# The first expert stage and the linear attention run as one stage, in slots of two tiles

## The chip, the cores and the metric

The kernel runs on one core of a Trainium2 chip. A core has TensorE for matrix products (PE in the profile, PEld for its weight loads), VectorE (DVE), ScalarE (ACT), GpSimd (POOL) and SyncE (SP), which here issues the transfers. Each engine works through its own instructions in order, and they meet through semaphores. The metric is the device time of one execution in microseconds; lower is better. Three runs of the kernel before gave 2261.31, 2261.96 and 2263.22 us, a median of 2261.96 us.

## The reference, cut to what matters

Four layers follow each other on x of 4 batches x 1024 tokens x 128 features. The change concerns the second and third step, of layers 0 and 1:

```
# experts of layer 0: E = 20, K = 2, H = 32
h = gelu(xf @ wg1 + bg1);  logits = (h @ wg2 + bg2)[:, :E]
probs = softmax(logits);   top_vals, top_idx = top_k(probs, 2)
gates = zeros(N, E) with top_vals at top_idx
y = sum over e of gates[:, e] * (xf @ We[e] + be[e])      # every expert is computed for every token
x = layernorm(x + y)
# linear attention of layer 1
Xn = layernorm(x) * g + b;  Q, K, V = split(Xn @ W_in.T)
Q, K = rotary(Q), rotary(K)                               # on the first 64 features
A = sum over all 1024 tokens of l2norm(K) * V             # one row of 128 per batch
Y = (A * l2norm(Q)) @ W_out.T
x = layernorm(x + (Y + x))
```

Everything is fp32. The sum A is over a whole batch, so no output of the attention exists before all eight tiles of its batch have gone through the experts.

## The kernel before, in words

A batch is eight tiles of 128 tokens; x lies with the tokens on the partitions. Every stage is a block of its own: all engines meet at a barrier at its end, and the stages hand x on through DRAM.

**The expert stage** (`gelu_gated_experts_stage`, tiles named moe_) works in slots w of two tiles; a batch has four, which are called k = 0 to 3 here. In a slot TensorE multiplies the two tiles by 20 experts in five fills n = 0 to 4 of four experts each (L892, one bank of 128x512 per fill and tile, four banks `outs` in turn). Fills 0 and 2 are taken by ScalarE, which scales each expert's 128x128 by its gate into `scaled` (L729, 8 experts), and GpSimd adds these up in halves (`add_scaled`, L682 and L684). Fills 1, 3 and 4 are taken by VectorE, which adds gate times product to `r` (L805, 12 experts). `close` (L813, then L204 and L207) adds GpSimd's sum and takes the moments, GpSimd makes 1/std (L223, L224), and `normalise` (L216) writes the tile. `close(w-1)` stands in slot w behind the first vector fill, `normalise(w-1)` behind the last. Routing (`route`, `gate`) of batch b+1 is done in slots 2 and 3 of batch b.

**The attention stage** (`linear_attention_stage`, tiles named lin_) takes a batch at a time, in a loop on the hardware: norm of eight tiles, transposes, product with W_in into K, Q, their swapped pairs and V (L1126), squares and copy on ScalarE (L1042, L1044), the rotation on VectorE (L1073 to L1077, four operations per tile), one over the lengths on GpSimd (L224 on 128x16), the sum over keys (L1140), W_out scaled by it (L1080), the product with it (L1149), two residual additions, norm, and the store.

Of the kernel before, what the change touches and what calls it, by code (L numbers as in the profile page):

```python
# [17 lines left out]
P = 128  # L18
# [534 lines left out]
def gelu_gated_experts_stage(nc, x_in, x_out, fetched):  # L553
# [15 lines left out]
    SCALAR_FILLS = (0, 2)  # L569
    VECTOR_FILLS = (1, 3, 4)  # L570
    ON_SCALAR = len(SCALAR_FILLS) * PER_FILL
    with ExitStack() as ctx:
        m = Room(ctx, nc, "moe0")
        wg1, bg1, wg2, we, be, ident = (fetched.at[n] for n in ("wg1", "bg1", "wg2", "we", "be", "ident"))
        power = m.sb("power", [P, 2]); eps = m.sb("eps", [P, 2])
# [4 lines left out]
        chosen = m.sb("chosen", [P, TILES, E]); total = m.sb("total", [P, TILES]); inv = m.sb("inv", [P, TILES])  # L580
# [4 lines left out]
        rstd = m.sb("rstd", [P, 2]); y = m.sb("y", [P, 2, PER_HALF, P])  # L585
        to_act = [m.psum(f"to_act{i}", [P, HALF]) for i in range(2)]
        outs = [m.psum(f"outs{i}", [P, HALF]) for i in range(4)]
        logit_bank = m.psum("logit_bank", [P, HALF])
        bias_bank = m.psum("bias_bank", [P, 2 * P])

        built = m.sem("built")
        x_loaded = [m.sem(f"x_loaded{i}") for i in range(2)]; stored = [m.sem(f"stored{i}") for i in range(2)]
        A = m.ring("A", to_act, 0)
        logits_full, shifted_ready, exps_ready, gates_ready = (
            m.sem(n) for n in ("logits_full", "shifted_ready", "exps_ready", "gates_ready"))
        bias_full, outs_full, added, scaled_ready, pool_added = (
            m.sem(n) for n in ("bias_full", "outs_full", "added", "scaled_ready", "pool_added"))
        moments_ready, rstd_ready, y_ready = (m.sem(n) for n in ("moments_ready", "rstd_ready", "y_ready"))
        dve_steps, pool_steps = m.sem("dve_steps"), m.sem("pool_steps")

# [4 lines left out]

        def additions():

            order = []
            for w in range(PAIRS):
                order.append(("begin", w))  # L610
# [8 lines left out]
        def fills_of_A():  # L619

            fills = []
            for b in range(B):
                fills += [("xT", b, g) for g in range(HALVES)] + [("hT", b, g) for g in range(HALVES)]
                fills += [("gT", b, g) for g in range(HALVES)]
            return fills

        A_FILLS = {fill: n for n, fill in enumerate(fills_of_A())}

        def taken_from_A(what, b, g):
            return A.free.value(0, A_FILLS[what, b, g] + 1)  # L630

        def tiles_of(w):
            b, k = divmod(w, PER_BATCH)
            return b, [2 * k, 2 * k + 1]

# [14 lines left out]
        def _(sp):  # L650

            def load(b):
                after(sp, added, ADDED["begin", (b - 1) * PER_BATCH - 1] if b > 1 else 0)
                sp.dma_start(x[:, b % 2], x_in[b]).then_inc(x_loaded[b % 2], 16)

            def store(g):
                b, half = divmod(g, HALVES)
                sp.wait_ge(y_ready, 2 * (g + 1))
                sp.dma_start(x_out[b][:, half * PER_HALF:(half + 1) * PER_HALF, :], y[:, g % 2]).then_inc(stored[g % 2], 16)
# [3 lines left out]
            for g in range(B * HALVES):  # L663
                if g % HALVES == 1 and g // HALVES + 2 < B:
                    load(g // HALVES + 2)
                store(g)
            for i in range(2):
                sp.wait_ge(stored[i], 16 * B)

        @block.gpsimd  # L670
        def _(pool):
# [3 lines left out]
            pool.wait_ge(built, 3)  # L675

            def add_scaled(w):
# [8 lines left out]
            def rsqrt(w):  # L686
                pool.wait_ge(moments_ready, w + 1)
                rsqrt_on_pool(steps, pool, rstd[:], moments[:, :, 1], plus_eps[:], eps[:], power[:]).then_inc(rstd_ready, 1)
# [2540 lines left out]
```

## Time and profile before

| what | us |
|---|---|
| median of three runs | 2261.96 |
| the profiled execution's own time | 2276.37 |
| its span | 2274.5 |
| expert stage, from the first load to the attention stage's first load | 282.77 to 485.95 |
| attention stage, from there to the next stage's first load | 485.95 to 628.33 |

| engine | busy us over the whole span | share |
|---|---|---|
| PE | 1954.7 | 86% |
| DVE | 1663.7 | 73% |
| ACT | 1097.9 | 48% |
| POOL | 545.5 | 24% |

Shares over the whole span mix eight stages. The two stages of the change take 345.56 us of it, and they are read from their own stretches in the rows below.

### The profile page before, as it was taken

How to read it: one execution, taken by the hardware profiler on the slowest of the kernel's cores; microseconds unless marked ns; L12 is line 12 of the kernel's file. 1: busy time of each engine (PE TensorE's matmuls, PEld its weight loads, DVE VectorE, ACT ScalarE, POOL GpSimd, SP SyncE). 2: the span in 40 equal slices, each digit the busy share in tenths (PEclk: the TensorE clock that was granted, in tenths of full speed). 3: DMA queues.
4: the chain of work that ended last, by engine and by line, in shares of the span. 5: the costliest groups of instructions: out<-in, count | busy, mean ns of one | idle time of the engine just before them, and what ended most of it. 6: DMA issues, size and time to landing. Idle time of an engine off the chain costs nothing. (4 is left out here: it accounts for less than half of the span.)

```text
span 2274.5 us, 31782 instructions
## 1 busy us (share of the span) xinstructions
PE 1954.7 (86%) x10146; PEld 1263.0 (56%) x10146; DVE 1663.7 (73%) x4032; ACT 1097.9 (48%) x2397; POOL 545.5 (24%) x624
## 2 busy tenths in 40 slices
PE   8999799956589999489999999998679988893997
PEld 5666644424367777357666766666453444443544
DVE  4555458866628888668899899888444989996576
ACT  3433345533245555166566666555204756663343
POOL 2222124432201222200000000000001777775111
PEclk9999989976689999689999999999858999996888
DMA  2000000020120000000000000000310222222100
GB/s 84 28 28 18 12 29 21 15 101 28 47 95 10 10 20 10 10 19 1 6 15 6 1 15 6 1 6 6 138 63 9 54 56 70 60 62 73 38 28 28
DMA packets 37238, 75.30 MB, mean 33 GB/s; under 512 B 8822, under 2 KB 20286, under 8 KB 36342
## 3 DMA queue, kind: packets, MB, share of 16 engines
q1 hardware_dynamic: 28918, 56.89, 7.2%
q0 software_dynamic: 8192, 16.79, 2.8%
q8 instruction: 69, 1.13, 0.2%
q14 instruction: 59, 0.48, 0.1%
HBM read 58.98 MB, written 14.68 MB: 32 GB/s over the span
## 5 line engine op out<-in xcount | busy, mean ns | idle before, releaser
L1965 ACT ACTIVATE pk_sums<-pk_sum 128x512 f32<-128x512 f32 x448 | 243.3, 596 | 227.1 <-PE pk_sum L2191 214.6
L2067 DVE SCALAR_TENSOR_TENSOR pk_level<-pk_sums,pk_least 128x1024 f32<-128x1024 f32 x256 | 324.0, 1276 | 22.5 <-ACT pk_sums L1965 21.3
L2198 PE MATMUL pk_weights<-product_keys_early_ident,pk_level 128*128 128x128 f32 x2048 | 267.4, 273 | 35.8 <-DVE pk_level L2067 35.8
L2419 POOL DMA_INDIRECT tk_values<-top_keys_values,tk_index x256 | 243.7, 952 | 202.3 <-DVE tk_index L2584 124.8
L2198 PEld LDWEIGHTS pk_weights<-product_keys_early_ident,pk_level 128*128 128x128 f32 x2048 | 232.0, 141 | 102.0 <-issue 66.5
L2735 PE MATMUL tk_to_act<-tk_keys,tk_xT 128*128 128x512 f32 x512 | 236.7, 610 | 30.1 <-ACT tk_scores L2484 29.4
L2735 PEld LDWEIGHTS tk_to_act<-tk_keys,tk_xT 128*128 128x128 f32 x512 | 95.8, 195 | 153.0 <-issue 93.8
L2190 PE MATMUL pk_sum<-pk_lay_rows,pk_partsT 96*128 96x512 bf16 x448 | 170.2, 380 | 0.2 <-ACT pk_sums L1965 0.2
L2191 PE MATMUL pk_sum<-pk_lay_columns,pk_partsT 96*128 96x512 bf16 x448 | 169.2, 378 | 0.0
L1647 PEld LDWEIGHTS er_outs<-experts_early_w,er_hT 128*128 128x128 f32 x1024 | 134.0, 192 | 59.8 <-issue 56.4
L2582 DVE MAX8 tk_best<-tk_scores 128x8 f32<-128x4096 f32 x32 | 141.3, 4416 | 14.9 <-ACT tk_scores L2484 14.9
L892 PE MATMUL moe_outs<-experts_early_we,moe_xT 128*128 128x512 f32 x320 | 150.7, 611 | 0.3
L2484 ACT ACTIVATE tk_scores<-tk_to_act 128x512 f32<-128x512 f32 x256 | 135.5, 597 | 16.5 <-PE tk_to_act L2735 16.3
L2584 DVE FIND_INDEX8 tk_index<-tk_best,tk_scores 128x8 uint32<-128x4096 f32 x32 | 141.4, 4419 | 0.0
L1647 PE MATMUL er_outs<-experts_early_w,er_hT 128*128 128x128 f32 x1024 | 134.5, 275 | 0.0
L1636 PE MATMUL er_to_act<-er_xT,experts_early_w 128*128 128x512 f32 x256 | 133.4, 603 | 0.0
L1349 ACT ACTIVATE er_hT<-er_to_act,experts_early_b 128x512 f32<-128x512 f32 x128 | 85.6, 687 | 93.1 <-PE er_to_act L1636 92.2
L223 POOL TENSOR_TENSOR pk_plus_eps<-pk_moments,pk_eps 128x4 f32<-128x4 f32 x8 | 8.2, 1030 | 496.2 <-DVE pk_moments L207 496.2
L805 DVE SCALAR_TENSOR_TENSOR moe_r<-moe_outs,moe_gates,moe_r 128x128 f32<-128x128 f32 x384 | 104.8, 342 | 24.2 <-PE moe_outs L892 22.9
L729 ACT ACTIVATE moe_scaled<-moe_outs,moe_gates 128x128 f32<-128x128 f32 x256 | 69.7, 382 | 74.3 <-PE moe_outs L892 74.3
L892 PEld LDWEIGHTS moe_outs<-experts_early_we,moe_xT 128*128 128x128 f32 x320 | 57.6, 192 | 73.4 <-issue 48.5
L2723 PE MATMUL tk_to_dve<-tk_values,tk_ident 128*128 128x128 f32 x512 | 68.6, 292 | 23.3 <-ACT tk_values L2472 21.8
(398 smaller groups left out, 3714.4 us busy)
## 6 DMA issues: line engine op xcount, KB each, us to landing
tk_scores<-top_keys_compress SPq DMA_DIRECT2D x1, 4096.0 KB, 15.1
tk_values<-top_keys_values,tk_index POOLq DMA_INDIRECT x256, 2.5
att_x_proj<-x_first SPq DMA_DIRECT2D x4, 512.0 KB, 5.0
att_x_res<-x_first SPq DMA_DIRECT2D x4, 512.0 KB, 4.1
x_after_attention<-att_y SPq DMA_DIRECT2D x4, 512.0 KB, 4.7
moe_x<-x_after_attention SPq DMA_DIRECT2D x4, 512.0 KB, 3.9
x_after_experts<-moe_y SPq DMA_DIRECT2D x8, 256.0 KB, 2.0
lin_x<-x_after_experts SPq DMA_DIRECT2D x4, 512.0 KB, 4.3
```

Of the source, the lines that this page charges most:

```text
L892: pe.matmul(outs[f % len(outs)][:], xT[:, b % 2, t * P:(t + 1) * P], we[:, n * PER_FILL:(n + 1) * PER_FILL, :].rearrange("p e d -> p (e d) ...
L1647: ins = pe.matmul(bank[:, s * P:(s + 1) * P], hT[:, (t * CHUNKS + n) % (LAG + 1), s * P:(s + 1) * P], w2[:, n, :], start=k == 0 and s == 0 ...
L1965: act.activation(sums[:, n % SUMS, half * HALF:(half + 1) * HALF], bank[:], ACT.Copy).then_inc(S.free.sem, 1)
L2067: dve.scalar_tensor_tensor(level[:, n % LEVELS, :], sums[:, n % SUMS, :], least[:, t % 2, h:h + 1], sums[:, n % SUMS, :], ALU.is_ge, ALU.m ...
L2190: pe.matmul(bank[:], partsT[:, t % 3, i, :], lay_rows[:, half * HALF:(half + 1) * HALF], start=True, stop=False)
L2191: pe.matmul(bank[:], partsT[:, t % 3, i + 1, :], lay_columns[:], start=False, stop=True).then_inc(S.full.sem, 1)
L2198: ins = pe.matmul(weights[:, ch * P:(ch + 1) * P], level[:, n % LEVELS, ch * P:(ch + 1) * P], ident[:], is_transpose=True, start=h == 0 an ...
L2419: pool.indirect_dma_start(out=values[:, slot, k, :], out_offset=None, in_=c["values"], in_offset=bass.IndirectOffsetOnAxis(ap=index[slot][ ...
L2484: act.activation(scores[:, t % KEPT, ch * HALF:(ch + 1) * HALF], bank[:], ACT.Copy).then_inc(S.free.sem, 1)
L2582: steps.link(dve.max(best[:, slot, :], scores[:, t % KEPT, :]))
L2584: dve.max_index(index[slot][:], best[:, slot, :], scores[:, t % KEPT, :]).then_inc(index_ready, 1)
L2735: pe.matmul(bank[:], xT[:, b, at * P:(at + 1) * P], keys[:, ch * HALF:(ch + 1) * HALF], start=True, stop=True).then_inc(S.full.sem, 1)
```

## The change

The two stages become one block, `gated_experts_and_linear_attention_stage` (tiles named ml_). There are 16 expert slots and four more for the attention alone. In slot w the experts of pair w run, and beside them the norm of pair w-1's result and its second norm, the transposes and the product with W_in for pair w-2, and the rotation of pair w-3. The result of the experts stays on chip in `mid`. The part of the attention that needs a whole batch (`lengths`, `sum_keys`, `scale_out_weights`, `project_out`, `close_out`, `normalise_out`) runs in slots k = 2 and 3 of the next batch. The fills are dealt out anew: 0, 2 and 4 to ScalarE with GpSimd (12 experts), 1 and 3 to VectorE (8 experts). The weights of this attention and of the experts of layer 1 are loaded right behind the first two batches of x. In the diff the first loop over SLOTS is GpSimd's, the second VectorE's, and the last part is TensorE's, behind fill n of its slot.

```
-    SCALAR_FILLS = (0, 2)
-    VECTOR_FILLS = (1, 3, 4)
+    SCALAR_FILLS = (0, 2, 4)
+    VECTOR_FILLS = (1, 3)
+    SLOTS = PAIRS + PER_BATCH
+    KQV_TILES = 4
...
             load(0)
             load(1)
-            for g in range(B * HALVES):
...
+            for dst, src in loads:
+                sp.dma_start(dst[:], src).then_inc(consts, 16)
+            next_weights.load(sp)
...
                 n = ON_SCALAR // 2
-                while n > 1:
+                while n > 2:
                     steps.link(pool.tensor_tensor(own[:, :, 0:n, :], own[:, :, 0:n, :], own[:, :, n:2 * n, :], ALU.add))
                     n //= 2
-                pool.tensor_tensor(own[:, :, 0, :], own[:, :, 0, :], own[:, :, 1, :], ALU.add).then_inc(pool_added, 1)
+                steps.link(pool.tensor_tensor(own[:, :, 0, :], own[:, :, 0, :], own[:, :, 1, :], ALU.add))
+                pool.tensor_tensor(own[:, :, 0, :], own[:, :, 0, :], own[:, :, 2, :], ALU.add).then_inc(pool_added, 1)
...
+            for w in range(SLOTS):
+                b, k = divmod(w, PER_BATCH)
+                if valid(w - 2):
+                    mid_root(w - 2)
+                if k == 2 and b > 0:
+                    lengths(b - 1)
+                if k == 3 and b > 0:
+                    root2(b - 1, 0)
+                if valid(w - 1):
+                    add_scaled(w - 1)
+                if k == 3 and b > 0:
+                    root2(b - 1, 1)
+                if valid(w - 1):
+                    root(w - 1)
...
+            for w in range(SLOTS):
+                b, k = divmod(w, PER_BATCH)
+                more = b + 1 < B
+                if valid(w):
+                    begin(w)
+                if valid(w - 2):
+                    normalise_mid(w - 2)
+                if valid(w - 3):
+                    rotate(w - 3)
+                if valid(w):
+                    add_outs(w, VECTOR_FILLS[0])
+                if k == 3 and b > 0:
+                    normalise_out(b - 1, 0)
+                    close_out(b - 1, 1)
+                if valid(w - 1):
+                    close(w - 1)
+                if more and k == 2:
+                    route(b + 1)
+                if more and k == 3:
+                    gate(b + 1)
+                if valid(w):
+                    add_outs(w, VECTOR_FILLS[1])
+                if k == 2 and b > 0:
+                    scale_out_weights(b - 1)
+                if valid(w - 1):
+                    normalise(w - 1)
+                    measure_mid(w - 1)
+                if k == 2 and b > 0:
+                    close_out(b - 1, 0)
+                if k == 3 and b > 0:
+                    normalise_out(b - 1, 1)
...
+                    if n == 1 and valid(w - 2):
+                        transpose_xn(w - 2)
+                    if n == 2 and valid(w - 3):
+                        transpose_q(w - 3)
+                    if n in (2, 3) and valid(w - 2):
+                        project_in(w - 2, n - 2)
+                    if more and k == 2 and n == 3:
+                        route(b + 1)
+                    if k == 2 and n == 3 and b > 0:
+                        sum_keys(b - 1)
+                    if k == 2 and n == 4 and b > 0:
+                        project_out(b - 1, 0)
+                    if k == 3 and n == 1 and b > 0:
+                        project_out(b - 1, 1)
```

The new functions hold the operations of the old attention stage on two tiles instead of eight. The waits that matter: `normalise_mid(w)` on VectorE waits for `mid_root(w)` on GpSimd and that for `measure_mid(w)` on VectorE; `close(w)` waits for `add_scaled(w)`, and that for ScalarE's last fill of slot w; on TensorE fill 3 waits for VectorE's fill 1, fill 0 of the next slot for VectorE's fill 3, and `transpose_q(w)` for `rotate(w)`.

VectorE before, a plain slot of the expert stage, from one `close` to the next (moe_r is the running sum, moe_y the result):

```order
L813 TENSOR_TENSOR moe_r<-moe_r,moe_scaled 128x256
L204 BN_STATS moe_stats<-moe_r 128x6 x2
L207 BN_AGGR moe_moments<-moe_stats 128x2 x2
L805 SCALAR_TENSOR_TENSOR moe_r<-moe_outs,moe_gates,moe_r 128x128 x16
L216 TENSOR_SCALAR moe_y<-moe_r,moe_moments,moe_rstd 128x128 x2
L784 TENSOR_TENSOR moe_r<-moe_bias_bank,moe_x 128x256
L805 SCALAR_TENSOR_TENSOR moe_r<-moe_outs,moe_gates,moe_r 128x128 x8
```

VectorE in the changed kernel, the same stretch in a plain slot (L947 is `close`, L939 `add_outs`, ml_mid the experts' result, ml_xn its second norm, L978 to L981 the rotation of one tile):

```order
L947 TENSOR_TENSOR ml_r<-ml_r,ml_scaled 128x256
L939 SCALAR_TENSOR_TENSOR ml_r<-ml_outs,ml_gates,ml_r 128x128 x8
L216 TENSOR_SCALAR ml_mid<-ml_r,ml_moments,ml_rstd 128x128 x2
L204 BN_STATS ml_mid_stats<-ml_mid 128x6 x2
L207 BN_AGGR ml_mid_moments<-ml_mid_stats 128x2 x2
L918 TENSOR_TENSOR ml_r<-ml_to_dve,ml_x 128x256
L216 TENSOR_SCALAR ml_xn<-ml_mid,ml_mid_moments,ml_mid_rstd 128x128 x2
L978 TENSOR_TENSOR ml_turned<-ml_kqv,ml_cos 128x128
L979 TENSOR_TENSOR ml_turned<-ml_kqv,ml_sin 128x128
L980 TENSOR_TENSOR ml_kqv<-ml_turned 128x2x64
L981 TENSOR_TENSOR ml_kv<-ml_kqv 128x128
```

Eight of the 24 expert additions of a slot are gone; a second norm and the rotation of two tiles (the last four rows stand twice) stand between the two groups of additions.

GpSimd before, a slot: three additions and the root.

```order
L682 TENSOR_TENSOR moe_scaled<-moe_scaled 128x2x512
L682 TENSOR_TENSOR moe_scaled<-moe_scaled 128x2x256
L684 TENSOR_TENSOR moe_scaled<-moe_scaled 128x2x128
L223 TENSOR_TENSOR moe_plus_eps<-moe_moments,moe_eps 128x2
L224 TENSOR_TENSOR moe_rstd<-moe_plus_eps,moe_power 128x2
```

GpSimd in the changed kernel, a slot k = 2 with the lengths of the batch before (ml_plus_eps_l):

```order
L223 TENSOR_TENSOR ml_mid_plus_eps<-ml_mid_moments,ml_eps 128x2
L224 TENSOR_TENSOR ml_mid_rstd<-ml_mid_plus_eps,ml_power 128x2
L223 TENSOR_TENSOR ml_plus_eps_l<-ml_norms,ml_eps_l 128x16
L224 TENSOR_TENSOR ml_inv<-ml_plus_eps_l,ml_power 128x16
L753 TENSOR_TENSOR ml_scaled<-ml_scaled 128x2x768
L753 TENSOR_TENSOR ml_scaled<-ml_scaled 128x2x384
L755 TENSOR_TENSOR ml_scaled<-ml_scaled 128x2x128
L756 TENSOR_TENSOR ml_scaled<-ml_scaled 128x2x128
```

The additions are larger and one more, and the root of the second norm stands ahead of them.

## Rows read from the trace of the kernel before

**Rows 1.** Busy time by stretch: span, PE, PEld, DVE, ACT, POOL, granted clock, DMA share, GB/s.

```profile
390.00:434.00 44.00, 43.86 (x128) 19.27 (x126) 37.64 (x139) 23.41 (x73) 19.60 (x20) 1.00 0.03 13
540.00:570.00 30.00, 20.39 (x64) 12.95 (x63) 20.49 (x91) 10.90 (x44) 7.39 (x9) 0.67 0.15 50
```

**Rows 2.** Groups of instructions, 282.5 to 628: busy us, mean ns | idle before.

```profile
L805 DVE SCALAR_TENSOR_TENSOR moe_r<-moe_outs,moe_gates,moe_r 128x128 f32<-128x128 f32 x384 | 104.8, 342 | 24.2 <-PE moe_outs L892 22.9
L729 ACT ACTIVATE moe_scaled<-moe_outs,moe_gates 128x128 f32<-128x128 f32 x256 | 69.7, 382 | 74.3 <-PE moe_outs L892 74.3
L682 POOL TENSOR_TENSOR moe_scaled<-moe_scaled 128x1024 f32<-128x1024 f32 x16 | 37.6, 2347 | 25.8 <-ACT moe_scaled L729 25.6
L682 POOL TENSOR_TENSOR moe_scaled<-moe_scaled 128x512 f32<-128x512 f32 x16 | 20.3, 1271 | 1.3
L684 POOL TENSOR_TENSOR moe_scaled<-moe_scaled 128x256 f32<-128x256 f32 x16 | 11.6, 727 | 1.3
```

**Rows 3.** Instructions by time, expert stage: start us, us taken, instruction.

```profile
299.71 10.93 PE L892 MATMUL moe_outs<-experts_early_we,moe_xT 128*128 128x512 f32 x20
346.94 9.14 PE L892 MATMUL moe_outs<-experts_early_we,moe_xT 128*128 128x512 f32 x20
352.67 0.43 DVE L813 TENSOR_TENSOR moe_r<-moe_r,moe_scaled 128x256 f32<-128x256 f32 x1
353.65 0.25 DVE L207 BATCH_NORM_AGGREGATE moe_moments<-moe_stats 128x2 f32<-128x6 f32 x2
354.25 0.71 POOL L224 TENSOR_TENSOR moe_rstd<-moe_plus_eps,moe_power 128x2 f32<-128x2 f32 x1
```

**Rows 4.** The same view: VectorE beside GpSimd's additions.

```profile
354.93 3.70 POOL L682 TENSOR_TENSOR moe_scaled<-moe_scaled 128x1024 f32<-128x1024 f32 x2
358.28 1.24 DVE L216 TENSOR_SCALAR moe_y<-moe_r,moe_moments,moe_rstd 128x128 f32<-128x128 f32 x2
358.71 0.73 POOL L684 TENSOR_TENSOR moe_scaled<-moe_scaled 128x256 f32<-128x256 f32 x1
...
294.86 0.32 DVE L766 TENSOR_TENSOR moe_shifted<-moe_logits,moe_best 128x160 f32<-128x160 f32 x1
376.22 3.69 POOL L682 TENSOR_TENSOR moe_scaled<-moe_scaled 128x1024 f32<-128x1024 f32 x2
379.48 0.60 DVE L766 TENSOR_TENSOR moe_shifted<-moe_logits,moe_best 128x160 f32<-128x160 f32 x1
```

**Rows 5.** The same view: the rotation beside GpSimd's root of the lengths.

```profile
512.96 2.91 POOL L224 TENSOR_TENSOR lin_inv<-lin_plus_eps,lin_power 128x16 f32<-128x16 f32 x1
513.25 0.28 DVE L1074 TENSOR_TENSOR lin_turned<-lin_kqv,lin_sin 128x128 f32<-128x128 f32 x1
```

**Rows 6.** The same view: routing and gates; first operation of two tiles' rotation.

```profile
293.72 0.33 DVE L762 COPY moe_logits<-moe_logit_bank 128x160 f32<-128x160 f32 x1 [8.69 <-PE moe_logit_bank L867]
296.37 0.33 DVE L776 TENSOR_TENSOR moe_gates<-moe_chosen,moe_inv 128x160 f32<-128x160 f32 x1
...
603.35 0.28 DVE L1073 TENSOR_TENSOR lin_turned<-lin_kqv,lin_cos 128x128 f32<-128x128 f32 x1
604.40 0.28 DVE L1073 TENSOR_TENSOR lin_turned<-lin_kqv,lin_cos 128x128 f32<-128x128 f32 x1
```

**Rows 7.** The same view: end of the attention stage, last batch.

```profile
606.92 3.48 PE L1140 MATMUL lin_to_dve<-lin_inv,lin_kv 128*128 128x1 f32 x16
613.00 1.13 DVE L1090 SCALAR_TENSOR_TENSOR lin_once<-lin_to_dve,lin_inv,lin_x_res 128x128 f32<-128x128 f32 x4 [2.26 <-PE lin_to_dve L1149]
615.79 0.38 DVE L207 BATCH_NORM_AGGREGATE lin_moments<-lin_stats 128x2 f32<-128x6 f32 x4
617.63 1.11 DVE L216 TENSOR_SCALAR lin_y<-lin_r,lin_moments,lin_rstd 128x128 f32<-128x128 f32 x4 [1.46 <-POOL lin_rstd L224]
623.35 1.11 DVE L216 TENSOR_SCALAR lin_y<-lin_r,lin_moments,lin_rstd 128x128 f32<-128x128 f32 x4 [1.40 <-POOL lin_rstd L224]
628.33 1.51 SPq L1277 DMA_DIRECT2D er_x<-x_after_attention  x3
```

More of the change, by code:

```diff
@@ L687, in rsqrt, with root @@
+                pool.tensor_tensor(own[:, :, 0, :], own[:, :, 0, :], own[:, :, 2, :], ALU.add).then_inc(pool_added, 1)
+            def root(w):
                 pool.wait_ge(moments_ready, w + 1)
-                rsqrt_on_pool(steps, pool, rstd[:], moments[:, :, 1], plus_eps[:], eps[:], power[:]).then_inc(rstd_ready, 1)
-            for w in range(PAIRS):
-                if w > 0:
-                    rsqrt(w - 1)
-                add_scaled(w)
-            rsqrt(PAIRS - 1)
+                rsqrt_on_pool(steps, pool, rstd[:], moments[:, :, 1], plus_eps[:], eps[:, 0:2], power[:, 0:2]).then_inc(rstd_ready, 1)
@@ new lines, in root2 @@
+            def root2(b, g):
+                pool.wait_ge(moments2_ready, b * HALVES + g + 1)
+                rsqrt_on_pool(steps, pool, rstd2[:], moments2[:, :, 1], plus_eps2[:], eps[:], power[:, 0:PER_HALF]).then_inc(rstd2_ready, 1)
+            for w in range(SLOTS):
+                b, k = divmod(w, PER_BATCH)
+                if valid(w - 2):
[10 more added lines that the diff above has]
+                    root(w - 1)
@@ new lines, in normalise_mid, with rotate @@
+            def normalise_mid(w):
+                b, tiles = tiles_of(w)
+                dve.wait_ge(mid_rstd_ready, w + 1)
+                if w >= 2:
+                    dve.wait_ge(A.free.sem, taken_from_A("xnT", w - 2, 0))
+                norm_apply(dve, xn[:, w % 2], mid[:, b % 2, pair_of(w), :], mid_moments[:, w % 2], mid_rstd[:, w % 2]).then_inc(xn_ready, 1)
+            def rotate(w):
+                b, tiles = tiles_of(w)
+                if w == 0:
+                    dve.wait_ge(consts, 16 * len(loads))
+                for i, t in enumerate(tiles):
+                    dve.wait_ge(A.free.sem, taken_from_A("kqv", w, i))
+                    after(dve, kv_ready, 2 * w + i - 1)
+                    own = kqv[:, (2 * w + i) % KQV_TILES, :]
+                    first, second = (turned[:, i, part, :].rearrange("p (a n) -> p a n", a=2) for part in (0, 1))
+                    rotating = own[:, 0:2 * P].rearrange("p (a n) -> p a n", a=2)[:, :, 0:ROT]
+                    steps.do(dve.tensor_tensor(first, rotating, cos[:, t, :].rearrange("p (a n) -> p a n", a=2), ALU.mult))
+                    steps.link(dve.tensor_tensor(turned[:, i, 1, :], own[:, 2 * P:2 * P + 2 * ROT], sin[:, t, :], ALU.mult))
+                    steps.link(dve.tensor_tensor(rotating, first, second, ALU.add))
+                    dve.tensor_tensor(kv[:, b % 2, t, :], own[:, 0:P], own[:, 3 * P:4 * P], ALU.mult).then_inc(kv_ready, 1)
@@ new lines, in scale_out_weights, with close_out @@
+            def scale_out_weights(b):
+                dve.wait_ge(V.full.sem, V.to_take(0))
+                bank = V.take()
+                dve.tensor_scalar(w_sum[:], w_out[:], bank[:, 0:1], None, ALU.mult).then_inc(V.free.sem, 1)
+            def close_out(b, g):
+                dve.wait_ge(V.full.sem, V.to_take(0))
+                bank = V.take()
+                dve.wait_ge(inv_ready, b + 1)
+                after(dve, r2_ready, b * HALVES + g)
+                for i in range(PER_HALF):
+                    t = g * PER_HALF + i
+                    last = dve.scalar_tensor_tensor(once[:, i * P:(i + 1) * P], bank[:, i * P:(i + 1) * P],
+                                                    inv[:, b % 2, Q, t:t + 1], mid[:, b % 2, t, :], ALU.mult, ALU.add)
+                last.then_inc(V.free.sem, 1)
+                dve.wait_ge(V.free.sem, taken_from_V("out", b, g))
+                after(dve, y_ready, b * HALVES + g)
+                dve.tensor_tensor(r2[:].rearrange("p t d -> p (t d)"), once[:],
+                                  mid[:, b % 2, half_of(g), :].rearrange("p t d -> p (t d)"), ALU.add).then_inc(r2_ready, 1)
+                dve.wait_ge(r2_ready, b * HALVES + g + 1)
+                norm_stats(steps, dve, r2[:], stats2[:], moments2[:]).then_inc(moments2_ready, 1)
@@ L823, in _, with normalise_out @@
+            def normalise_out(b, g):
+                dve.wait_ge(rstd2_ready, b * HALVES + g + 1)
+                after(dve, stored[g], 16 * b)
+                norm_apply(dve, y[:, g], r2[:], moments2[:], rstd2[:]).then_inc(y_ready, 1)
             route(0)
             gate(0)
-            for w in range(PAIRS):
+            for w in range(SLOTS):
                 b, k = divmod(w, PER_BATCH)
                 more = b + 1 < B
-                begin(w)
-                for n in range(FILLS):
-                    if n in VECTOR_FILLS:
-                        add_outs(w, n)
-                    if n == VECTOR_FILLS[0] and w > 0:
-                        close(w - 1)
-                    if n == VECTOR_FILLS[-1] and w > 0:
-                        normalise(w - 1)
-                    if more and k == 2 and n == 3:
-                        route(b + 1)
-                    if more and k == 3 and n == 1:
-                        gate(b + 1)
```

483 lines of the change are left out of this document (203 added, 280 removed).

## The prediction

> **What bounds the kernel now.** I first read the page's busy time in slices, then the busy time by stretch, which splits the two stages. In the expert stage a batch takes 44 us and PE is busy 43.86 of them at the full granted clock: PE bounds it, VectorE at 37.64 has little room left [rows 1]. In the attention stage a batch takes 30 us and no engine is busy more than 20.49; PE was granted 0.67 on the mean [rows 1]. It is a chain of waits from engine to engine. Laid beside each other the two would fill each other's gaps. By load a batch would need, on VectorE, 37.64 + 20.49 less 32 additions of 0.273 (104.8/384) = 49.4 us; on ACT 23.41 + 10.90 + 32 scalings of 0.272 = 43.0; on PE 43.86 + 13.7 (20.39 at 0.67) = 57.5; on POOL about 37 [rows 1, 2]. Before, a batch costs 44 + 30 = 74. So by load alone some 17 us a batch could go. But each engine works in order, and what decides is the chain that closes from one slot to the next.
>
> **The prices.** `add_scaled` now adds 1536, 768, 256 and 256 elements per partition. The rows have 1024 at 2.347, 512 at 1.271 and 256 at 0.727, which is 2.10 ns per element: 3.42 + 1.81 + 0.73 + 0.73, with three gaps of 0.08 (358.63 to 358.71) 6.93 us, where it was 4.5 [rows 2, 4]. The first is shown by no row; it is at least the 2.35 of 1024 and at most 1.5 times it, 3.52; I take 3.42, from the slope. `close` with its moments is 352.67 to 353.90, 1.25. From the moments to GpSimd's root is 353.90 to 354.96, 1.08 with the wait [rows 3]. Eight additions are 2.2, two multiplications of a norm 0.6 (1.11 for four), two tiles' moments 0.8 (the later part of `close`) [rows 2, 3, 7]. The rotation is 1.05 a tile, 2.2 for two, 1.7 of it behind the second operation; routing with gates is 293.72 to 296.70, 2.98, of which 0.2 waits, so 1.7 and 1.1 [rows 6]. `close_out` of a half is 613.00 to 616.17, 3.2; its root 1.46; its norm 1.11 [rows 7]. The lengths are 2.9 and 0.4 of addition, 3.4 with the hand-over [rows 5].
>
> **VectorE does not run beside GpSimd's additions.** This is the term on which the sign rests. Two VectorE multiplications of a norm began at 358.28, while GpSimd was adding until 358.63. They took 1.24 instead of 0.6: the first ended 0.08 behind that addition and the second 0.08 behind the next one, at 359.52 against 359.44. An addition with both inputs in SBUF on 160 elements took 0.32 alone and 0.60 where GpSimd was adding until 379.91; it ended at 380.08 [rows 4]. So an operation of these kinds waits for the GpSimd addition that is under way, and one slips through at each border between two. `add_outs`, which reads PSUM and one SBUF tile, is untouched: 342 ns on the mean in a stage where GpSimd adds 40% of the time [rows 2]. Before, little met this. Now `normalise_mid` (2 operations) and `rotate` (8, all with both inputs in SBUF) are released by `mid_root`, at the same moment as the 6.93 us of `add_scaled`. GpSimd has nothing between its root and the addition, so it goes first. Four of the ten operations pass at the four borders, and six of the rotation, 1.7 us, come behind.
>
> The Trainium skill, "SBUF — State Buffer", section "Who interferes with whom", has the rule for this: an exclusive lock on the port pair that both engines share, taken by scalar forms in a two-port mode and met by any VectorE operation with two SBUF inputs while GpSimd reads SBUF. Where it is wider than the rows is the root: while GpSimd raised 16 elements to a power for 2.91 us, the rotation's second operation ran in its usual 0.28 [rows 5]. By the rule as written `lengths` would stop the rotation too, some 4 us in each of three slots, 12 us more than my sum; that is a rival below.
>
> **A plain slot, from one `close` to the next.** Let R be the end of the first group of additions in slot w; `close(w-1)` follows at once if GpSimd has finished. 1.25 for `close`, 2.2 for the second group (with 0.5 for the second tile of fill 3, which TensorE can only begin at R: a fill of 128x512 is 9.14/10 = 0.9 us [rows 3]), 0.6 `normalise`, 0.8 `measure_mid`, 1.1 root: R + 6.5. Is ScalarE ready? PE: fill 3 two tiles 1.8, `project_in` 0.9, fill 4 1.8, and ScalarE half a tile pair more, 1.3: R + 5.8. Yes, just. Then 6.93 of additions, 1.7 of rotation, 2.3 of the first group: 17.4 us. Before it was 11.
>
> If TensorE is late by up to 3 us the rotation gets done ahead of the addition and the slot is 16.6 to 17.5, so this figure bends little.
>
> The others. Into k = 2: `lengths` lies ahead of `add_scaled`; in its 3.4 us norm and rotation pass, and the first group is under the addition: 6.5 + 3.4 + 6.93 + 0.1 = 16.9. From k = 2 to k = 3: 1.25, route 1.7, second group 2.2, W_out 0.3 and 0.6 and 0.8, `close_out(0)` 3.2 (10.1), root 1.4, addition 6.93, rest of the rotation 0.9, first group 2.3, `normalise_out` 1.1, `close_out(1)` 3.2: 26.0. From k = 3 to k = 0: 1.25 + gate 1.1 + 2.2 + 0.6 + 0.8 + 1.1 + 6.93 + 1.7 + 2.3 = 18.0. A full batch is 17.4 + 16.9 + 26.0 + 18.0 = 78.3 us, against 74 before.
>
> **The sum.** The beginning is as before until PE starts at 299.71; its ten fills end at 310.64, ScalarE 1.3 later, the addition 6.93 later: the first `close` at 319.0. Batch 0 has no attention behind it at first: 13.8, 18.5 and 18.0 for the next three, 369.3 [rows 3]. Two full batches: 525.9. The last has no routing and its last interval no expert additions behind: 17.4 + 16.9 + 24.3 + 14.7 = 73.3, so 599.2. The way out, pair 15 alone: `close` to the second norm 1.25 + 1.1 + 0.6 + 0.8 + 1.1 + 0.7 = 5.5; transposes, gain and shift, two products at the lower clock and ScalarE's last copy, about 5.2 (estimate: the same steps on eight tiles had two products at 0.9 each); lengths 3.5; from `sum_keys` to 613.00 6.1; from there to the last norm's end at 624.46 11.5; store and barrier 3.4 to 3.9: 35.2, so 634.4. Before it was 628.33 [rows 7]. The difference is +6.1: full batches of 78 instead of 74 and the long way out take what the stage switch between the two gives back.
>
> Nothing hangs on the transfers. The loads of weights are issued behind x(0) and x(1), and x(0) is asked for first; the store is 256 KB at a time with a slot or more of room. The cover for ScalarE is its 43 us in 78.
>
> For TensorE's clock: PE waits 4 us in a plain slot for the second norm (released only at the second border) and 5 to 6 us in slot 3 for gates and rotation. What stays low costs something where ScalarE's last fill comes late. Bounds: 0 (a slot bends little, above) and +30 (below). Nearest is 0, by the slack; I take +3. That makes +9 on the profiled 2276.37, 2285; the median lies 14 us lower than that execution, so 2262 + 9 = 2271.
>
> **Rivals.** (B) *VectorE runs beside GpSimd.* Should the norm and rotation pass freely, say because they get in ahead, then the addition is the loop: plain slot 6.5 + 6.93 = 13.4, batch 13.4 + 16.9 + 20.1 + 14.1 = 64.5, four batches and ends by the same count close at 551.5, stage end 586.7: 42 us less, 2220. Against it stand rows 4; for it, that no row has a rotation beside a long addition. (C) *TensorE's clock.* The attention stage had 0.67 with PE busy 68% [rows 1]. The new batch has PE work of 57.5 in 78, 73%. Below a granted mean of 57.5/78.3 = 0.73 PE itself becomes the longest, 86 us a batch at 0.67, 8 more, and the ends with it: +25 to +30, 2296. Against it, the waits are shorter than those of the attention stage. (D) *The root blocks as well*, the rule above: 2283. (E) *The slot does not close as I laid it*, PE ordering adds a wait that I have not seen, e.g. `transpose_gates` behind `gate`: within C's reach.
>
> **How the numbers follow.** My case 0.60, 2271, its own range 2258 to 2286 (each of 16 slots off by 0.8); B 0.17; C with E 0.17; D 0.06. The range is 2222 to 2298: it leaves out the lower half of B and the upper half of C. A change of 0.2%, 4.5 us, is about what a measurement of this kernel can tell from none. Below 2257.4: B, a fifth of my case and a bit, 0.32. Within: 0.14. Above: 0.54.
>
> **What would show it.** Right: `close` to `close` in plain slots near 17.4 us; the two multiplications into ml_xn take 3.4 and 1.8 instead of 0.33; four of ten waiting operations end 0.08 behind a GpSimd addition; first addition 3.42. Wrong: operations of the rotation at 0.29 in the middle of a GpSimd addition (B, slots of 13.4); a mean granted clock under 0.73 with PE without gaps (C); rotations held during the 2.9 us root (D); a stage end far from 634.

## The result, and the profile after

The changed kernel takes 2281.95 us (median of 4, 2278.14 to 2288.95) against 2262.1 (2261.31 to 2263.22): a ratio of 1.0091, 95% interval 1.0065 to 1.0117. It is slower by 0.9%. The profiled execution took 2288.95 us and is one of the four. Ratios here and below leave out two executions in a slower state: one of experiment 4's four, which took 2945.18 us, and one of number 5's ten.

By starts in the two traces, the merged stage begins at 283.7 us from the span's start (before 282.8) and the first load of the next stage is issued at 639.01, where it was 628.33 [rows 7]: 355.3 us instead of 345.6, +9.8. The attention stage ahead of it gave +0.9, the rest of the program +1.9: the span is 12.6 us longer. The medians lie 20 us apart, since the profiled execution of before stands 14 us above its median and that of after 7. The +1.9 says nothing of the change: from the next stage's first load to the end the trace of before has 1646.2 us, and those of the change and of experiments 1 to 4 below have 1636.1 to 1648.3, with the same program in that part.

The busy time by stretch of the changed kernel, two full batches from closing addition to closing addition (PE, PEld, DVE, ACT, POOL busy, then the granted clock):

```profile
375.10:454.34 79.24, 64.66 (x198) 30.74 (x197) 66.21 (x202) 45.06 (x158) 39.94 (x38) 0.91 0.04 14
454.34:532.60 78.26, 63.91 (x197) 30.34 (x197) 66.01 (x203) 44.30 (x154) 40.00 (x38) 0.91 0.02 7
```

A batch took 44 + 30 us before [rows 1] and takes 79.24 and 78.26 now. No engine is full. Of VectorE's 66 us a part is waiting inside operations, not work: the same operations were 58 in [rows 1], and should have become fewer. The view by time shows why (start, us taken, instruction; in brackets the idle time before it and what ended it). A plain slot, between two closing additions:

```profile
375.10 0.43 DVE L947 TENSOR_TENSOR ml_r<-ml_r,ml_scaled 128x256 f32<-128x256 f32 x1
...
381.93 5.30 POOL L753 TENSOR_TENSOR ml_scaled<-ml_scaled 128x1536 f32<-128x1536 f32 x2
382.00 5.31 DVE L216 TENSOR_SCALAR ml_xn<-ml_mid,ml_mid_moments,ml_mid_rstd 128x128 f32<-128x128 f32 x2 [0.66 <-POOL ml_mid_rstd L224]
...
387.24 0.28 DVE L978 TENSOR_TENSOR ml_turned<-ml_kqv,ml_cos 128x128 f32<-128x128 f32 x1
387.31 0.79 POOL L755 TENSOR_TENSOR ml_scaled<-ml_scaled 128x256 f32<-128x256 f32 x1
387.37 0.44 PE L196 MATMUL ml_to_act<-experts_early_ident,ml_xn 128*128 128x128 f32 x2 [2.42 <-DVE ml_xn L216]
387.44 0.81 DVE L979 TENSOR_TENSOR ml_turned<-ml_kqv,ml_sin 128x128 f32<-128x128 f32 x1
388.18 0.72 POOL L756 TENSOR_TENSOR ml_scaled<-ml_scaled 128x256 f32<-128x256 f32 x1
388.28 0.77 DVE L980 TENSOR_TENSOR ml_kqv<-ml_turned 128x128 f32<-128x128 f32 x1
389.08 0.29 DVE L981 TENSOR_TENSOR ml_kv<-ml_kqv 128x128 f32<-128x128 f32 x1
...
390.35 2.15 DVE L939 SCALAR_TENSOR_TENSOR ml_r<-ml_outs,ml_gates,ml_r 128x128 f32<-128x128 f32 x8
392.59 0.43 DVE L947 TENSOR_TENSOR ml_r<-ml_r,ml_scaled 128x256 f32<-128x256 f32 x1
```

The root ends, GpSimd goes on at once with its two long additions, and the second norm, 0.60 us of work (two of 0.3), starts 0.07 later and ends at 387.31, 0.08 behind the second addition. The rotation's first operation gets in at that border at its usual 0.28; the next two take 0.81 and 0.77 and end 0.15 behind the third and the fourth addition. TensorE stands 2.42 us for the norm. After the last addition five operations of the rotation are left, 389.08 to 390.35. Then VectorE can take TensorE's results. The slot takes 17.49 us.

In a slot k = 2 the power of the lengths stands between the root and the additions. The norm and all eight operations of the rotation pass beside it, and VectorE then waits 4.45 us for GpSimd's sum:

```profile
398.96 2.91 POOL L224 TENSOR_TENSOR ml_inv<-ml_plus_eps_l,ml_power 128x16 f32<-128x16 f32 x1
399.46 0.28 DVE L979 TENSOR_TENSOR ml_turned<-ml_kqv,ml_sin 128x128 f32<-128x128 f32 x1
```

### The profile page after: what moved, and what is told of

Its sections match the earlier page's. It is cut to its first block and busy times, and to the rows that moved or that the text cites. A ratio compares the mean times of both kernels' runs of the same rounds, so it can differ in the third digit from the quotient of the medians.

```text
span 2287.1 us, 31555 instructions
## 1 busy us (share of the span) xinstructions
PE 1949.6 (85%) x10138; PEld 1256.9 (55%) x10146; DVE 1686.4 (74%) x3904; ACT 1135.7 (50%) x2541; POOL 589.7 (26%) x662
## 5 line engine op out<-in xcount | busy, mean ns | idle before, releaser
L1098 PE MATMUL ml_outs<-experts_early_we,ml_xT 128*128 128x512 f32 x320 | 167.6, 657 | 3.0 <-DVE ml_r L939 3.0
L826 ACT ACTIVATE ml_scaled<-ml_outs,ml_gates 128x128 f32<-128x128 f32 x384 | 105.0, 384 | 46.3 <-PE ml_outs L1098 46.3
L1098 PEld LDWEIGHTS ml_outs<-experts_early_we,ml_xT 128*128 128x128 f32 x320 | 62.9, 208 | 76.8 <-issue 54.0
L753 POOL TENSOR_TENSOR ml_scaled<-ml_scaled 128x1536 f32<-128x1536 f32 (+1 forms) x32 | 84.3, 2633 | 35.2 <-ACT ml_scaled L826 34.0
```

Of the source, the lines that this page charges most:

```text
L1098: pe.matmul(outs[f % len(outs)][:], xT[:, b % 2, t * P:(t + 1) * P], we[:, n * PER_FILL:(n + 1) * PER_FILL, :].rearrange("p e d -> p (e d) ...
```

## Experiments

Each kernel was timed beside the kernel before on the same chip (1 to 4 on one, 5 to 7, 8 with 9, and 10 with 11 each on another). Times differ between chips, so ratios are compared, and the stage in the traces.

**1. Powers in place of the additions.** GpSimd's four additions become three powers of 16, 16 and 4 elements that nobody reads, of the same length; 11 of the 12 experts of ScalarE are left out of the sum.

```diff
-  own[..0:n..] = own[..0:n..] + own[..n:2n..]   (1536, 768, 256, 256 elements)
+  idle_out[:] = eps_l2[:] ** power[:]           (16, 16, 4 elements)
```

> The changed kernel, but GpSimd's four additions of a slot (6.9 us) are replaced by three powers on 16, 16 and 4 elements per partition (2.91 + 2.91 + 1.01 us by the rows, also 6.9 with the gaps), so that the waits and GpSimd's time stay and only the kind of operation goes. Eleven of the twelve experts of ScalarE's fills are left out of the sum. Theory (VectorE's operations on SBUF wait for a GpSimd addition and not for a power): plain slots fall from 17.5 to about 13.4 us, a full batch from 78 to about 65, the kernel to 2235 to 2245 us; ml_xn's two multiplications take 0.6 us together and the rotation 2.2. Rival (it is GpSimd's time in the loop, not the blocking): slots and time stay, 2275 to 2285.

Measured 2236.65 us against 2266.58, ratio 0.9866 (0.9849 to 0.9882), inside the range of the theory. The three powers keep GpSimd busy for 109.5 us in all, the four additions did for 108.0, and VectorE is not held. The second norm and the rotation in a slot k = 2 of this kernel, beside the power of the lengths, then the groups of the norm and of the first replacement power:

```profile
385.25 0.60 DVE L216 TENSOR_SCALAR ml_xn<-ml_mid,ml_mid_moments,ml_mid_rstd 128x128 f32<-128x128 f32 x2 [0.66 <-POOL ml_mid_rstd L224]
385.48 2.91 POOL L224 TENSOR_TENSOR ml_inv<-ml_plus_eps_l,ml_power 128x16 f32<-128x16 f32 x1
385.97 0.28 DVE L976 TENSOR_TENSOR ml_turned<-ml_kqv,ml_sin 128x128 f32<-128x128 f32 x1
...
L216 DVE TENSOR_SCALAR ml_xn<-ml_mid,ml_mid_moments,ml_mid_rstd 128x128 f32<-128x128 f32 x32 | 9.6, 343 | 7.2 <-POOL ml_mid_rstd L224 7.1
L751 POOL TENSOR_TENSOR ml_idle_out<-ml_eps_l,ml_power 128x16 f32<-128x16 f32 x16 | 46.4, 2903 | 38.2 <-ACT ml_scaled L823 38.2
```

The norm is back at 343 ns on the mean. The stage is 315.7 us instead of 355.3, so what the additions cost beyond their own time is about 40 us of this stage. The ratio fell by more, by 0.0225 or some 50 us; 6 us more of the difference between the two traces lie in the unchanged rest, which differs by as much between other traces. One rival is left: the size changed with the operation. A replacement power reads 16 elements of each input, the first addition 1536. Whether it is the kind of operation or the amount it reads that lets VectorE pass was not tested.

**2. Merged, with the deal of before. 3. The new deal, not merged.** Fills (0, 2) to ScalarE and (1, 3, 4) to VectorE in the merged stage; (0, 2, 4) and (1, 3) in the kernel before.

```diff
-    SCALAR_FILLS = (0, 2, 4)      # 2: the other way round in 3, on the kernel before
-    VECTOR_FILLS = (1, 3)
+    SCALAR_FILLS = (0, 2)
+    VECTOR_FILLS = (1, 3, 4)
```

> One stage, but experts dealt as in the kernel before: 8 by ScalarE with GpSimd, 12 by VectorE. GpSimd's additions fall to 4.5 us a slot. Theory: the slot is serial, so what GpSimd saves (2.4 us) VectorE spends on 8 more additions (2.2), and one operation fewer passes at a border: plain slots 17.0 to 17.6, time 2276 to 2286. Rival (GpSimd's long additions alone are the loss): 2.4 us less in each of 16 slots, about 2243.

> The kernel before with two stages; only the deal is changed to 12 experts by ScalarE with GpSimd and 8 by VectorE. Theory: PE bounds these slots at 11 us and the loop over GpSimd's 6.9 us is two slots long (close 1.25, second group 2.2, ten fills 10, last scaling 1.3, additions 6.9: 21.7), so slots stay at 11 to 11.3 and only the last slot's longer addition shows: 2261 to 2268. Rival (the deal itself makes the slot longer, whatever the stage): 13 us a slot, about 2295.

Measured: 2, 2291.38 us, ratio 1.0109 (1.0092 to 1.0126), 5 us above the range of its theory, with the plain slots inside it (17.3 to 17.7) and the norms held as well (1201 ns each). 3, 2293.11 us, ratio 1.0118 (1.0101 to 1.0135): my expectation was wrong and the rival's 2295 right, with slots of 10.4 to 14.5 us where they were 9.7 to 12.9. I had laid out GpSimd's loop and left out what runs beside it. In this trace the norm at the end of a slot of the expert stage meets the longer addition, and TensorE then waits for banks:

```profile
362.40 5.32 POOL L682 TENSOR_TENSOR moe_scaled<-moe_scaled 128x1536 f32<-128x1536 f32 x2 [0.88 <-ACT moe_scaled L730]
362.59 5.21 DVE L216 TENSOR_SCALAR moe_y<-moe_r,moe_moments,moe_rstd 128x128 f32<-128x128 f32 x2
370.41 2.84 PE L893 MATMUL moe_outs<-experts_early_we,moe_xT 128*128 128x512 f32 x6 [1.65 <-DVE moe_r L806]
```

So each half of the change costs about 1.1% alone, and both together 0.9%. From first load to first load the two stages take 345.5 us before, 363.4 in number 2, 370.8 in number 3 and 355.3 with both: on top of the new deal the merge gains 15.5 us, on top of the old one it costs 17.9. In all three traces norms wait for additions; why the costs do not add up was not taken apart.

**4. Routing behind the second group.** `route(b + 1)` stands behind `add_outs` of fill 3 and `measure_mid` instead of ahead of them.

```diff
-                if more and k == 2:
-                    route(b + 1)
                 ...
                     add_outs(w, VECTOR_FILLS[1])
+                if more and k == 2:
+                    route(b + 1)
```

> The changed kernel with route(b+1) on VectorE behind the second group of additions instead of ahead of it. In the changed kernel VectorE stood 5.9 us before the routing of batch 1, because in slot 2 nothing had made close late. Theory: the interval from slot 2 to slot 3 falls from 23.9 to 18.5, the same interval of later batches (26.3) stays, and the kernel is 5 us faster: about 2275 to 2277. Rival (TensorE's routing is late for another reason, and the wait moves with it): no change, 2280 to 2283.

Measured 2286.31 us, ratio 1.0089 (1.0069 to 1.0109), no different from the change. The slot with the routing in batch 0 took 21.80 instead of 23.85 us, not 18.5: VectorE now waited 2.28 us for TensorE's fill 3 and 0.84 for the logits, and later slots gave the 2 us back (the next stage's first load is at 640.0).

**5 and 6. VectorE's SBUF work kept out of the additions.** VectorE's slot is written anew; GpSimd starts adding only behind the second norm. Number 6 is the same without that wait.

```diff
   VectorE, slot w:
-  close(w-1), route, add_outs(w, 3), normalise, measure_mid, begin, normalise_mid, rotate, add_outs(w+1, 1)
+  close(w-1), rotate, normalise, route, normalise_mid, measure_mid, add_outs(w, 3), begin, add_outs(w+1, 1)
   GpSimd:
+  after(pool, xn_ready, w - 1)                  # in add_scaled; not in 6
```

> The merged stage with the same deal of experts and the same additions on GpSimd, but written so that they meet nothing that waits for them. VectorE's slot is: closing addition, moments, rotation, normalise_mid, normalise, route (these it ran into the additions until now), and only then its expert additions out of TensorE's results, the opening addition and the LayerNorm of the middle's moments; GpSimd starts its additions only when VectorE has finished the normalise of the slot (one wait more, on xn). TensorE's and ScalarE's work on a slot moves one slot later where it needs the rotation, so the stage has one slot more (21). Theory (the loss of the change is VectorE's SBUF operations waiting for GpSimd's additions, some 5 us in each of 16 slots and more in those with the routing): GpSimd and VectorE then form a loop of 6.93 (additions) + 1.25 (root) + 2.2 (normalise and its wait) + some 1.2 of signals, about 11.8 us, below TensorE's 12 to 15, a batch takes 60 to 66 us instead of 78, and the next stage starts at 590 to 610: 2222 to 2245 us in all. Rival (the loss is the sum of work that the merge gives to one slot of VectorE and TensorE, or their clock, not the order beside GpSimd): the batches stay at 74 to 79 us and the extra slot adds some 10: 2270 to 2295.

> The same order without the wait of GpSimd for xn: its additions start as soon as ScalarE's last expert is there. Theory (additions block VectorE wherever they meet): where ScalarE is done before VectorE's rotation and normalise are, the additions fall on these, normalise then waits up to 5.3 us for a border, and the slot gets 1 to 5 us longer than with the wait: 2230 to 2265 us, with TENSOR_SCALARs of 5 us in the normalise's line where the other has 0.3. Rival (the order of VectorE's own program is all that counts, and a wait on GpSimd's path only lengthens the loop): this one is equal or faster than the one with the wait, by up to 1 us in a slot.

> The changed kernel again, unchanged, on the same chip as the two above, so that they are compared with it directly: 2278 to 2289 us, a ratio of 1.009 to the kernel before, with plain slots of 17.5 us and batches of 78 to 79 us, if the loss belongs to the program and not to the chip on which it was first timed.

The cut above shows VectorE and the wait alone. In both kernels TensorE's and ScalarE's order is changed too, GpSimd's root of the second norm comes behind its additions, and the stage has 21 slots for 20. So the gain over the change belongs to all of this together; number 6 against number 5 changes one thing.

On this chip the stage of the top keys took 581 to 584 us in the three traces, from its first load of x to the next stage's, where it took 467 to 476 in those of the change and of experiments 1 to 4. Medians were 2369.32 us for number 5, 2378.24 for number 6 and 2386.74 for the change again, against 2379.02. Ratios to before: number 5 0.9948 (0.9917 to 0.9978), number 6 0.9997 (0.9978 to 1.0015), the change again 1.0035 (1.0010 to 1.0059). The change is slower here too, but by less than the 1.009 expected; why was not tested. It does not lie in the merged stage, which took 358.7 us here and 355.3 in the first trace. TensorE's first product of the next stage came at 645.1 us (642.2 in the first trace of the change), at 620.2 in number 5 and at 625.6 in number 6. On a third chip number 5 again:

> The kernel with the new order of VectorE and GpSimd again, unchanged, beside the one above and perhaps on another chip than in its first run, where the stage of the top keys took 566 us in place of some 460 in all kernels. If its gain belongs to the program, the next stage starts at 620 us from the span's start (before 631.6) and the ratio is 0.992 to 0.997 again; on a chip where the stage of the top keys is short the time is some 2250 us. Rival (the gain hangs on that chip): the same or slower than before, 0.998 to 1.005.

2259.75 us against 2267.05, ratio 0.9966 (0.9957 to 0.9976), the next stage's first product at 619.0. The theory's mechanism holds. The groups of the second norm and of the rotation's last operation, of the change and then of number 5 (busy us, mean ns, idle before); in number 6 the second norm kept its 341 ns, and the first norm stands in its place:

```profile
L216 DVE TENSOR_SCALAR ml_xn<-ml_mid,ml_mid_moments,ml_mid_rstd 128x128 f32<-128x128 f32 x32 | 50.5, 1617 | 6.7 <-POOL ml_mid_rstd L224 6.6
L981 DVE TENSOR_TENSOR ml_kv<-ml_kqv 128x128 f32<-128x128 f32 x32 | 20.6, 644 | 1.1
```

```profile
L216 DVE TENSOR_SCALAR ml_xn<-ml_mid,ml_mid_moments,ml_mid_rstd 128x128 f32<-128x128 f32 x32 | 9.6, 341 | 0.0
L988 DVE TENSOR_TENSOR ml_kv<-ml_kqv 128x128 f32<-128x128 f32 x32 | 9.3, 292 | 1.1
```

```profile
L216 DVE TENSOR_SCALAR ml_mid<-ml_r,ml_moments,ml_rstd 128x128 f32<-128x128 f32 x32 | 13.7, 472 | 2.2 <-POOL ml_rstd L224 2.2
L987 DVE TENSOR_TENSOR ml_kv<-ml_kqv 128x128 f32<-128x128 f32 x32 | 15.5, 485 | 1.1
```

The 41 us of waiting norms are gone in number 5. Without the wait on GpSimd 6 us are back in the stage (339.5 us against 333.4), on the first norm and the rotation; that is the way the theory has it, but less than its 1 to 5 us in each slot, and no first norm took 5 us (the longest 1.9). The forecast of the size failed: full batches, between the closing additions of slots 4, 8 and 12, took 74.7 and 70.3 us, not 60 to 66, and the first of them is in the rival's range of 74 to 79. Here is number 5 in its slot with the key sums, VectorE and TensorE, and below the dots two rows of the same slot one batch later:

```profile
404.07 2.13 DVE L946 SCALAR_TENSOR_TENSOR ml_r<-ml_outs,ml_gates,ml_r 128x128 f32<-128x128 f32 x8
405.99 3.19 PE L1105 MATMUL ml_outs<-experts_early_we,ml_xT 128*128 128x512 f32 x4 [1.17 <-DVE ml_r L946]
408.98 3.41 PE L1129 MATMUL ml_to_dve<-ml_inv,ml_kv 128*128 128x1 f32 x16
412.25 2.06 PE L1118 MATMUL ml_to_act<-ml_w_in,ml_xnT 128*128 128x512 f32 x2
414.09 3.26 PE L1105 MATMUL ml_outs<-experts_early_we,ml_xT 128*128 128x512 f32 x4
416.10 0.35 DVE L946 SCALAR_TENSOR_TENSOR ml_r<-ml_outs,ml_gates,ml_r 128x128 f32<-128x128 f32 x1 [9.58 <-PE ml_outs L1105]
...
482.48 1.84 PE L1129 MATMUL ml_to_dve<-ml_inv,ml_kv 128*128 128x1 f32 x16
486.24 0.35 DVE L946 SCALAR_TENSOR_TENSOR ml_r<-ml_outs,ml_gates,ml_r 128x128 f32<-128x128 f32 x1 [5.04 <-PE ml_outs L1105]
```

VectorE frees the banks of fill 3 last, TensorE comes to fill 1 of the next slot through those banks, and between fills 0 and 1 it had other work. With GpSimd out of the way this loop of two engines is what VectorE waits for. But half of this wait is TensorE's clock: granted 0.66 from 404 to 412 us and 0.67 from there to the slot's end, and 1.00 in the same slot one batch later. There the key sums took 1.84 us instead of 3.41, VectorE waited 5.04 instead of 9.58, and the slot took 18.47 us instead of 23.49. The trace of number 5 on the third chip has the same two slots, 23.49 and 18.46. Why the clock is low in one of them is open.

**8. TensorE's order too.** Number 5 with what stood between fills 0 and 1 put behind fill 1. Two more edits go with it: the next batch's hidden layer a slot earlier and its routing a fill earlier on TensorE.

```diff
-            if n in (0, 1) and valid(w - 3):
-                out.append(("kqv", w - 3, n))
+            if n == 1 and valid(w - 3):
+                out += [("kqv", w - 3, 0), ("kqv", w - 3, 1)]
-                    if k == 3 and n == 0 and b > 0:
+                    if k == 3 and n == 1 and b > 0:
                         sum_keys(b - 1)
...
-            if more and k == 2 and n in (0, 1):
-                out.append(("hT", b + 1, n))
+            if more and k == 1 and n == 4:
+                out += [("hT", b + 1, 0), ("hT", b + 1, 1)]
...
-                    if more and k == 2 and n == 3:
+                    if more and k == 2 and n == 2:
                         route(b + 1)
```

> The new order of VectorE and GpSimd with a second correction, on TensorE. Its trace in the run before showed a loop of TensorE and VectorE instead of the loop of GpSimd that I had forecast: VectorE's closing addition stands behind its additions of expert group 1 of the next slot, TensorE comes to that group only once VectorE has freed the banks of group 3, and between groups 0 and 1 TensorE ran a projection (1.03 us) and in one slot of a batch the sum of the keys (3.41 us); VectorE waited 9.58 us there. Here both projections, the sum of the keys and the last output projection stand behind group 1, the next batch's hidden layer is one slot earlier and its routing one group earlier (VectorE had waited 1.53 us for it). Nothing else is changed. Theory (TensorE's order between the banks that it frees late and group 1 sets the slot): plain slots 13 to 14 us instead of 13.9 to 15.5, the slot with the keys 18 to 20 instead of 23.5, batches 62 to 68 instead of 70 to 75: the next stage starts 15 to 30 us earlier, a ratio to the kernel before of 0.980 to 0.990. Rival (the sum of TensorE's and VectorE's work is what bounds these slots, so what is moved behind group 1 comes back as a later group 2): batches within 1 us of the run before, a ratio of 0.993 to 0.997.

Measured 2242.52 us against 2267.05, ratio 0.9891 (0.9872 to 0.9909), beside number 5 on the same chip. Full batches took 68.7 and 68.3 us instead of 74.7 and 70.3. That is the theory's ratio, but not its slots. The slot with the key sums took 15.48 us in both batches, instead of 23.49 at the low clock and 18.47 at the full one, so the order itself is worth 3 us there and the clock was the other 5. The slot ahead of it got 3 us longer (17.46 and 17.78 for 14.63 and 14.62), as the rival has it. Of the 17 us by which the stage is shorter than number 5's, 9 lie ahead of the first full batch, 8 in the two full ones and none behind them; which of the three edits gave the 9 was not tested. A batch of it (from the closing addition of slot 5 to that of slot 9) in the view by stretch:

```profile
389.83:458.86 69.03, 61.04 (x198) 30.93 (x197) 49.13 (x203) 43.88 (x154) 40.49 (x38) 0.93 0.05 16
```

VectorE does a batch in 49.13 us, where the change has it busy for 66; the load worked out in the prediction was 49.4. TensorE's first product of the next stage comes at 603.4, where it came at 631.6 before the change.

**10. The deal, once the order is right.** Number 8 with fills (0, 2) to ScalarE and (1, 3, 4) to VectorE, beside number 8 again.

> The merged stage in the order of the last experiment (VectorE's SBUF operations kept out of GpSimd's additions, TensorE's projections behind group 1), with the deal of the experts as it was before the change: 8 by ScalarE with GpSimd, 12 by VectorE. GpSimd's additions are 4.5 us instead of 6.93 in a slot, VectorE has 8 additions of 0.27 us more out of TensorE's results. Theory: in this order VectorE and TensorE form the loop that sets the slot (VectorE waits some 3.4 us in a slot for TensorE's results), and the 2.2 us of additions fall into this loop, behind group 3, so slots get 1 to 2 us longer: 2250 to 2275 us, a ratio of 0.993 to 1.003; the new deal is then worth having once the order is right. Rival (GpSimd's additions set the slot in this order too): 2.4 us less in a slot, the stage ends 20 to 35 us earlier than in the kernel with the new deal: 2205 to 2225 us, 0.972 to 0.982.

Measured 2342.53 us, ratio 0.9855 (0.9807 to 0.9903); number 8 again (expected 0.987 to 0.991, and 603 us) 2344.5, ratio 0.9881 (0.9811 to 0.9951), before 2381.35, with the next stage's first product at 594.7 and 603.8. The theory, that the new deal would be the better one, fell: in the traces the old deal's stage is 9 us shorter, while the two ratios can't be told apart. The rival's 20 to 35 us did not come either.

## Why the prediction was right

2271 was forecast, 2282 measured, inside the likeliest case's own range of 2258 to 2286 and for its reason. That the stage's end came within 5 us of the forecast is in part luck: terms that missed in both directions took each other off.

**The lock.** Right, and tested: additions hold VectorE (experiment 1 takes them away at the same length, experiments 5 and 6 move VectorE out of and into their way), powers on 16 elements don't (rival D out: its 4 us more in each slot k = 2 did not come, the slots took 16.22 and 16.23 us where 16.9 was forecast without them). The three plain slots, forecast at 17.4, took 17.49, 16.63 and 16.62 us, within the 16.6 to 17.5 that was given, but not for its reason: that range was for a TensorE that comes later, and in the short slots VectorE waited less for it (its second group ended 3.6 us behind the start of the closing addition, and 4.5 in the long one); the slots behind a k = 3 took 17.45, 19.26 and 19.15 for 18.0. The first two additions were forecast at 3.42 + 1.81 and took 5.30 together. Five operations of the rotation came late, not six: one more slipped in at the border at 387.24.

**The sum.** Forecasts in brackets: first closing addition 320.66 (319.0), first full batch from 375.10 (369.3), full batches 79.24 and 78.26 (78.3), last close 601.93 (599.2). Two terms were too low. Batch 0's slot with the routing took 23.85 us instead of 18.5. I had charged VectorE the 1.7 us of the routing's operations, but it stands ahead of the additions of fill 3 and waits there for TensorE, which has that product behind fill 3 and two projections:

```profile
337.96 1.02 PE L1111 MATMUL ml_to_act<-ml_w_in,ml_xnT 128*128 128x512 f32 x2
338.91 1.96 PE L1073 MATMUL ml_to_dve<-experts_early_wg,ml_hT 33*128 33x20 f32 x16
340.91 0.33 DVE L894 COPY ml_logits<-ml_to_dve 128x160 f32<-128x160 f32 x1 [5.88 <-PE ml_to_dve L1073]
```

In the later batches that wait is covered, since VectorE comes there later: 26.27 against 26.0. The other is the way out, 37.1 instead of 35.2, all of the excess ahead of the sum of the keys at 618.24 (16.3 us behind the last close, 14.2 forecast). Against these, the last four slots took 69.3 us in all, where 73.3 were forecast. The stage came to +9.8 against +6.1 worked out, or +9 with the allowance for the clock:

```profile
618.24 3.54 PE L1122 MATMUL ml_to_dve<-ml_inv,ml_kv 128*128 128x1 f32 x16 [1.55 <-issue]
624.30 1.12 DVE L995 SCALAR_TENSOR_TENSOR ml_once<-ml_to_dve,ml_inv,ml_mid 128x128 f32<-128x128 f32 x4 [2.19 <-PE ml_to_dve L1131]
639.01 1.72 SPq L1293 DMA_DIRECT2D er_x<-x_after_attention  x3
```

So the allowance of 3 us was near the miss in size, not for its reason: the granted clock was 0.91 in full batches and 0.58 only from 600 us on. Rival C is out by that; PE was busy 64 us a batch, which I had at 57.5, in batches of 79.24 and 78.26.

**From the profiled time to the median.** This term missed by most: "the median lies 14 us lower than that execution" was carried over, and is 7 us after. With 0.8 on the stage, the +1.9 of the rest and the +0.9 of the attention stage it makes the 11 us between 2271 and 2282. The 14 us were no property of the kernel that could be carried over. In the eleven kernels timed later the profiled execution stands between 11.9 us below its median (number 10) and 10.6 above (the change again), and the trace of before has 175.7 us in the last stage where that of the change has 169.0, with the same program there. The profiled execution of before was a long one.

**Rival B**, VectorE free beside GpSimd, forecast 2220 with plain slots of 13.4. Experiment 1 is that world by other means: plain slots of 12.6, 2237 on its chip. The batches there were 68.4, not 64.5: the routing slot took 22.3 us for 20.1 and the one behind it 16.3 for 14.1.

## What to carry to other kernels

Before moving additions to GpSimd, list the VectorE operations with SBUF inputs that are released at the same moment, and write them ahead of the additions. Here the same work went from 0.9% slower to 1.1% faster by order and one added wait. And when such a hold is gone, look for the next loop before promising its size: a bank that is freed late and the work that stands in front of the product that refills it. Compare the granted clock of two slots before putting a wait down to their order, and do not carry the distance of one profiled execution from its median over to another kernel.

## What the runs showed of the hardware

A GpSimd power on 16 elements takes 2.91 us and held none of the VectorE operations that ran beside it; GpSimd additions of the same total length cost this kernel's stage 40 us through VectorE. The Trainium skill, "SBUF — State Buffer", section "Who interferes with whom", says that a VectorE instruction with two SBUF inputs contends with a GpSimd instruction that reads SBUF. The additions here agree with it; the powers on 16 elements do not, since the rotation's operations took their usual 0.28 us beside one of 2.91. An operation that VectorE has waiting gets in at each border between two GpSimd additions and the one behind it waits for the next: a norm's multiplication took 1617 ns on the mean, and 341 with the order changed. Between chips, one stage with indirect loads took over 100 us longer (581 to 584 us for 467 to 476), while the merged stage of the same kernel differed by 3.4 us.
